# Self attention: the exponentials of four key blocks added on VectorE, one ones-matmul group for each sum

## The chip, the cores and the metric

The kernel runs on one core of one Trainium2 chip (trn2). The metric is device time in microseconds for one execution, the median of three runs; lower is better. Engines are named as in the profile: PE is TensorE's matmul, PEld its weight load, DVE VectorE, ACT ScalarE, POOL GpSimd, SP SyncE.

## What is computed

The reference is a decoder layer stack on x of shape (4, 512, 512): a self attention with rotary embedding, token-routed experts, a quantised MLP, a second self attention, a cross attention over a context and a last linear layer. Only the two self attentions matter here; each has 16 heads of 32 and runs for 4 batch elements of 512 tokens. Cut to that:

```python
q, k, v = (heads of a linear layer of layernorm(x))      # (4, 16, 512, 32) each
attn  = jnp.einsum('bhqd,bhkd->bhqk', q, k) * Dh ** -0.5 # the first one with rotary q and k
probs = jax.nn.softmax(attn, axis=-1)
out   = jnp.einsum('bhqk,bhkd->bhqd', probs, v)
x     = x + out.transpose(0, 2, 1, 3).reshape(B, S, D) @ out_w.T + out_b
```

The kernel computes exp(score - maximum), multiplies it by v without normalising, sums it over the keys, and multiplies the context by the reciprocal of the sum. The change is in how that sum over 512 keys is formed.

## The kernel before

Class `Attention` builds both self attentions (`rope` true for the first) and the cross attention (`cross`). All engines run their own instruction stream and meet at semaphores; the order on each engine is written out by hand. A batch element goes through projections (PE, with pieces of the maximum search planned between them), the output projection of the element before, the value projection, and then the stretch that this text calls the heads: `pe_heads` on PE, the loop over `u` in `act_batch` on ACT, `dve_self_heads` on DVE.

The heads are 16 units u, u = 4 g + kb: a group g of four heads (HG = 4) and one of T = 4 blocks of 128 keys. For a unit PE makes the scores of four heads (L1075, keys on the partitions), ACT takes their exponentials in two halves of 128x1024 fp32 (L1224, into one of three buffers `p(u)`), and PE multiplies them by the values (`pe_values`, L883), one unit behind. Keys lie on the partitions, so the sum over them takes a matmul with a matrix of ones (`pe_sum`, L897, four heads side by side into PSUM bank 7). Because that is fp32 work, DVE first adds the exponentials of two neighbouring units (`dve_add`, L1468, two halves) into one tile `pair_sum`, and `pe_pair_sum` takes the ones-matmul of the pair: two of them, accumulated, make a group's sum. A `pe_sum` is eight PE instructions in the trace.

Around a group's end the order is as follows. DVE adds at odd u. PE takes the first pair at kb = 3 and the second at kb = 1 of the next group, after the scores of that unit and the values of the one before; at the last group it comes after the next batch element's first projection, and in the last element right after the heads. Then DVE reads the sums by a transpose (`dve_read_sums`, L1319), before its add of the same unit; at kb = 2 it inverts and transposes them back (L1324, L1326) and multiplies the context (L1336); ACT and POOL split the result into a high and a low half (L1145, L1595). DVE also holds, at fixed units, the layer norm of the next element (L183, L194, L201), the low half of its transposed tiles (L1296, after units 8, 10, 12, 14), the transposed maxima (L1291) and, in the last element, weight splits (L456).

`pair_sum` is one buffer, so an add waits until the ones-matmul of the pair before has read it (`pair_read`); the exponential of u waits until the buffer of u - 3 has been added and multiplied by the values (`act_wait_block`).

Of the kernel before, what the change touches and what calls it, by code (L numbers as in the profile page):

```python
# [15 lines left out]
NB = 4  # L16
S = 512
D = 512
NH = 16
HD = D // NH  # L20
T = S // P
C = D // P
# [21 lines left out]
ALU = mybir.AluOpType  # L44
# [118 lines left out]
def slot(ap, i):  # L163

    return ap[:, bass.ds(i, 1), :].rearrange("p a n -> p (a n)")
# [72 lines left out]
class Phase:  # L238
# [22 lines left out]
    def pe(self, pe): pass  # L261
# [6 lines left out]
class Start(Phase):  # L268
# [56 lines left out]
    def pe(self, pe):  # L325
        m = self.m
        pe.wait_ge(*self.at(self.own_made, 1))
        pe.wait_ge(*self.at(self.memsets, 2))
        n = NE * NB * T
        pe.matmul(m.ps[:, 0, 0:n], self.tri, flat(self.own), start=True, stop=True)  # L330
        pe.matmul(m.ps[:, 1, 0:n], self.ones, flat(self.own), start=True, stop=True).then_inc(self.counted, 1)
        for i in range(T):
            pe.wait_ge(*self.at(self.norm.xn_ready, i + 1))
            self.following.pe_turn_x(pe, i, None)

        pe.wait_ge(*self.at(self.copied, 1))
        self.following.pe_first_chunk(pe)
# [143 lines left out]
class Attention(Phase):  # L481
# [15 lines left out]
    def __init__(self, m, name, mats, bufs, early, q_bias, k_bias, v_bias, out_bias, rope=False, cross=False):  # L497
# [24 lines left out]
        s = self.sem  # L522
# [66 lines left out]
        own = not cross  # L589
        self.out_full, self.out_free, self.out_added = s("out_full", own * NB * T), s("out_free", own * (NB - 1) * T), s("out_added", own * NB * T)  # L590
        self.values_done = s("values_done", own * NB * NH)
        self.paired, self.pair_read = s("pairs_added", own * NB * self.ADDS * 2), s("pair_sums_read", own * NB * self.ADDS)
        self.qs_ready = s("sin_part", rope * NB * self.NPROJ)
        self.sums_read, self.reciprocals, self.inverted = s("sums_read", NB * C), s("reciprocals", NB * C), s("sums_inverted", NB * C)
        self.normed, self.ch, self.cl = (s(n, NB * C) for n in ("ctx_normed", "ctx_high", "ctx_low"))
# [38 lines left out]


    PAIRS = HG * T // 2
    ADDS = NH // 2
    WITH_PROJ = ("", "", ",pp", ",pp", "p,pp", "p,pp", "m,pp", ",pp")
    WITH_OUT = (",pp", ",pp", "m,pp", "p,pp")
    WITH_V = ("p,pp", "m,pp", ",pp", ",pp")  # L640
# [260 lines left out]
    def pe_sums(self, pe, u, b):  # L901


        if self.cross:
            if u:
                self.pe_sum(pe, self.p(u - 1), u % T == 1, u % T == 0).then_inc(self.pv_done, 1)
        elif u < NH and u % T == T - 1:
            self.pe_pair_sum(pe, u // 2 - 1, b)
        elif T < u < NH and u % T == 1:
            self.pe_pair_sum(pe, (u - T) // 2 + 1, b)  # L910

    def pe_pair_sum(self, pe, n, b):
        if n % 2 == 0 and n:
            pe.wait_ge(*self.at(self.sums_read, b * C + n // 2))
        pe.wait_ge(*self.at(self.paired, 2 * (b * self.ADDS + n + 1)))
        self.pe_sum(pe, self.pair_sum, n % 2 == 0, n % 2 == 1).then_inc(self.pair_read, 1)

    def pe_proj(self, pe, n, b):
        m = self.m
# [15 lines left out]
    def pe(self, pe):  # L935
        if self.cross:
            self.pe_cross(pe)
            return
        if not self.rope:
            for i in range(T):  # L940
                self.pe_turn_x(pe, i, None)
            self.pe_first_chunk(pe)
        if self.rope:
            pe.wait_ge(*self.at(self.const, self.nconst))
        self.pe_batch(pe, 0)
        with pe.Fori(1, NB - self.rope) as b:
            self.pe_batch(pe, b)
        if self.rope:
            self.pe_batch(pe, NB - 1)
            self.pe_pair_sum(pe, self.ADDS - 1, NB - 1)  # L950
            self.pe_last_out(pe)
            return
        self.pe_pair_sum(pe, self.ADDS - 1, NB - 1)

        for c in range(C):
            if c == 0:
                pe.wait_ge(*self.at(self.cl, NB * C - 1))
            if c == C - 1:
                pe.wait_ge(*self.at(self.cl, NB * C))
            for i in range(T):  # L960
                last = self.pe_out(pe, i, [c])
                if c == C - 1:
                    last.then_inc(self.out_full, 1)
# [22 lines left out]
    def pe_batch(self, pe, b):  # L986
        first = first_of(b)
        self.of_batch(b)
        if not first:
            pe.wait_ge(*self.at(self.slot_free[0], self.slot_count(0, b)))  # L990
        for n in range(self.NPROJ):
            if n or not first:
                self.pe_proj(pe, n, b)
            if n == 0 and not first:
                self.pe_pair_sum(pe, self.ADDS - 1, b - 1)
            if self.rope and n:
                self.pe_rotate(pe, n - 1, b)
            self.pe_planned(pe, b, "proj", n, 1)
        if self.rope:
            self.pe_rotate(pe, self.NPROJ - 1, b)  # L1000
        if not first:
            self.weights.wait(pe, 3)
            pe.wait_ge(*self.at(self.cl, b * C))
            for i in range(T):
                self.wait_free(pe, ("v", i), b)
                self.pe_out(pe, i, [0, 1])
                self.pe_planned(pe, b, "out", i, 0)
                self.pe_out(pe, i, [2, 3]).then_inc(self.out_full, 1)
                self.pe_planned(pe, b, "out", i, 1)
        self.pe_project_values(pe, b)  # L1010
        self.pe_heads(pe, b)
# [89 lines left out]
    def act_wait_chunks(self, act, n, b):  # L1101

        if n < 2 and not self.cross and not first_of(b):
            if n == 0:
                act.wait_ge(*self.at(self.values_done, b * NH))
                act.wait_ge(*self.at(self.paired, 2 * b * self.ADDS))
            else:
                act.wait_ge(*self.at(self.pair_read, b * self.ADDS))

    def act_audio(self, act, n, c):  # L1110
        act.wait_ge(*self.at(self.audio_loaded, n * 16 + 16))
# [137 lines left out]
    def act_wait_block(self, act, u, h, b):  # L1249

        before = u - 3
        if u == 2:
            for half in range(2):
                act.wait_ge(*self.at(self.stacked[half], (b + 1) * 24 * 16))
        if before >= 0:
            act.wait_ge(*self.at(self.values_done, b * NH + before + 1))
            act.wait_ge(*self.at(self.paired, 2 * (b * self.ADDS + before // 2) + h + 1))

    def act_next(self, act, u):

# [50 lines left out]
    def dve_read_sums(self, v, g, b):  # L1311


        if self.cross:
            v.wait_ge(*self.at(self.pv_done, b * NH + T * (g + 1)))
        else:
            v.wait_ge(*self.at(self.pair_read, b * self.ADDS + 2 * g + 2))
        v.wait_ge(*self.at(self.normed, b * C + g))
        v.transpose(self.sums, self.m.ps[:, 7, :]).then_inc(self.sums_read, 1)  # L1319

# [135 lines left out]
                self.dve_planned(v, b, "v", i, step)  # L1456
        self.dve_self_heads(v, b)

    def dve_add(self, v, n, b):

        if n == 0:
            for half in range(2):
                v.wait_ge(*self.at(self.stacked[half], (b + 1) * 24 * 16))
        v.wait_ge(*self.at(self.pair_read, b * self.ADDS + n))
        for h in range(2):
            cols = slice(2 * h * S, (2 * h + 2) * S)
            v.wait_ge(*self.at(self.exp_done[h], b * NH + 2 * n + 2))
            v.tensor_tensor(self.pair_sum[:, cols], self.p(2 * n)[:, cols], self.p(2 * n + 1)[:, cols], ALU.add).then_inc(self.paired, 1)  # L1468

    def dve_self_heads(self, v, b):  # L1470
        m = self.m
        first = first_of(b)
        nb = (b + 1) % NB
        own = lambda i: slot(m.x, nb * T + i)
        for u in range(NH):
            g, kb = divmod(u, T)
            self.dve_planned(v, b, u - 1, 3)
            for step in range(3):
                self.dve_planned(v, b, u, step)
            if g and kb == 1:  # L1480
                self.dve_read_sums(v, g - 1, b)
            if u % 2:
                self.dve_add(v, u // 2, b)
            if g and kb == 2:
                self.dve_multiply(v, g - 1, b)
            if self.of_last(b):
                self.dve_next(v, u)
            if u == (3 if self.rope else 0) and not self.without_next(b):
                if self.rope:
                    v.wait_ge(*m.x_all)  # L1490
                self.norm.dve_stats(v, own, (0, 1))
            if u == (4 if self.rope else 0) and not self.without_next(b):
                self.norm.dve_stats(v, own, (2, 3))
                self.norm.dve_aggregate(v, b)
            if self.rope and not first:
                if u == 0:
                    self.dve_final_moments(v, b - 1)
                if u == 2:
                    self.dve_final_apply(v, b - 1)
            for i in range(T):  # L1500
                if not self.without_next(b) and u == ((6, 6, 8, 8) if self.rope else (4, 4, 6, 6))[i]:
                    self.norm.dve_apply(v, b, own, lambda i: m.xn[:, i, :], [i])
# [226 lines left out]
def first_of(b):  # L1729

    return isinstance(b, int) and b == 0
# [890 lines left out]
```

## Time and profile before

| | us |
|---|---|
| median of three runs | 1719.95 (1714.42 to 1724.76) |
| the profiled execution | 1716.46 |
| its span, first to last instruction | 1714.5 |
| busy in the span: PE / DVE / ACT / POOL | 1489.2 / 1261.1 / 871.7 / 530.4 |
| mean granted TensorE clock, share of full | 0.958 |

Busy time is the union of an engine's instructions; PE's matmuls are pipelined and their ends modelled. The idle time in a row is that of the engine just before the instruction, with what ended it behind the arrow. The profiled execution lies 3.5 us below the median of the runs.

### The profile page before, as it was taken

How to read it: one execution, taken by the hardware profiler on the slowest of the kernel's cores; microseconds unless marked ns; L12 is line 12 of the kernel's file. 1: busy time of each engine (PE TensorE's matmuls, PEld its weight loads, DVE VectorE, ACT ScalarE, POOL GpSimd, SP SyncE). 2: the span in 40 equal slices, each digit the busy share in tenths (PEclk: the TensorE clock that was granted, in tenths of full speed). 3: DMA queues.
4: the chain of work that ended last, by engine and by line, in shares of the span. 5: the costliest groups of instructions: out<-in, count | busy, mean ns of one | idle time of the engine just before them, and what ended most of it. 6: DMA issues, size and time to landing. Idle time of an engine off the chain costs nothing. (4 is left out here: it accounts for less than half of the span.)

```text
span 1714.5 us, 26624 instructions
## 1 busy us (share of the span) xinstructions
PE 1489.2 (87%) x8760; PEld 577.9 (34%) x8761; DVE 1261.1 (74%) x1783; ACT 871.7 (51%) x1071; POOL 530.4 (31%) x450
## 2 busy tenths in 40 slices
PE   3789999999959994688798999999999999999948
PEld 1223323233236661344332323333242323323213
DVE  4687897878855556888687788788945776768675
ACT  2245273452822333788737455463837454563735
POOL 1625447355420004422141322323131321414130
PEclk9889999999979997899998999999999999999979
DMA  5241202103313446300230201212031120303002
GB/s 196 74 122 32 68 25 52 47 0 75 119 54 111 147 135 137 54 1 0 62 74 1 54 22 31 84 65 65 25 91 33 45 53 24 73 0 92 12 0 99
DMA packets 82776, 105.40 MB, mean 61 GB/s; under 512 B 14096, under 2 KB 56208, under 8 KB 82576
## 3 DMA queue, kind: packets, MB, share of 16 engines
q1 hardware_dynamic: 79120, 96.10, 19.3%
q0 software_dynamic: 3584, 8.39, 2.3%
q8 instruction: 39, 0.64, 0.2%
q14 instruction: 33, 0.27, 0.1%
HBM read 48.21 MB, written 18.35 MB: 39 GB/s over the span
## 5 line engine op out<-in xcount | busy, mean ns | idle before, releaser
L1224 ACT ACTIVATE arena<-ps 128x1024 f32<-128x1024 f32 x384 | 373.4, 1026 | 108.4 <-PE ps L1075 98.0
L1284 DVE TENSOR_REDUCE arena<-ps 128x2 f32<-128x1024 f32 x256 | 299.7, 1220 | 56.2 <-PE ps L828 56.0
L468 PE MATMUL ps<-xt,w 128*128 128x512 f16 (+1 forms) x1872 | 295.3, 308 | 7.6 <-DVE w L456 3.8
L1075 PE MATMUL ps<-arena 97*128 97x512 f16 (+1 forms) x768 | 211.8, 389 | 14.8 <-ACT arena L1224 10.6
L883 PE MATMUL ps<-arena 128*32 128x512 f32 x1536 | 208.5, 615 | 15.3 <-DVE arena L1319 8.7
L468 PEld LDWEIGHTS ps<-xt,w 128*128 128x128 f16 (+1 forms) x1872 | 151.4, 99 | 141.7 <-issue 36.5
L468 PE MATMUL ps<-w,arena 128*128 128x512 f16 (+1 forms) x804 | 185.5, 381 | 12.7 <-issue 12.7
L1468 DVE TENSOR_TENSOR arena<-arena 128x1024 f32<-128x1024 f32 x128 | 175.2, 1408 | 11.8 <-PE ps L897 9.9
L1725 POOL TENSOR_TENSOR arena<-arena 128x512 f16<-128x512 f32 x96 | 116.6, 1216 | 158.3 <-ACT arena L1204 148.4
L1199 ACT ACTIVATE arena<-ps,arena 128x512 f32<-128x512 f32 x96 | 65.9, 687 | 182.2 <-PE ps L468 171.9
L1581 DVE TENSOR_SCALAR arena<-arena 128x1024 f32<-128x1024 f32 x128 | 106.7, 839 | 68.4 <-ACT arena L1224 67.9
L897 PE MATMUL ps<-arena 128*32 128x512 f32 x1024 | 138.0, 610 | 12.6 <-DVE arena L1468 11.8
L1595 POOL TENSOR_TENSOR arena<-arena 128x512 f16<-128x512 f32 x36 | 56.4, 1566 | 276.5 <-ACT arena L1145 276.5
L1075 PEld LDWEIGHTS ps<-arena 97*128 97x128 f16 (+1 forms) x768 | 59.2, 98 | 198.2 <-issue 100.9
L468 PEld LDWEIGHTS ps<-w,arena 128*128 128x128 f16 x804 | 75.7, 98 | 108.6 <-issue 30.5
L1135 ACT ACTIVATE arena<-ps 128x512 f32<-128x512 f32 x48 | 28.7, 597 | 136.7 <-PE ps L468 136.7
L468 PE MATMUL ps<-w,xt 128*128 128x512 f16 x384 | 92.0, 380 | 0.0
L828 PE MATMUL ps<-arena 32*128 32x512 f16 x512 | 70.0, 394 | 23.9 <-DVE arena L1284 21.7
L2071 PE MATMUL ps<-arena 128*128 128x512 f16 x256 | 63.3, 401 | 27.7 <-ACT arena L2089 27.7
L201 DVE TENSOR_SCALAR xn<-x,mv,rstd 128x512 f32 (+1 forms) x76 | 63.6, 890 | 24.4 <-POOL rstd L214 24.4
L2053 PE MATMUL ps<-arena,xt 128*128 128x512 f16 x256 | 61.9, 399 | 14.1 <-DVE arena L2212 9.4
L211 POOL TENSOR_TENSOR rstd<-mv,eps 128x4 f32<-128x4 f32 x27 | 9.8, 363 | 189.1 <-DVE mv L194 180.1
(217 smaller groups left out, 2001.5 us busy)
## 6 DMA issues: line engine op xcount, KB each, us to landing
arena<-arena SPq DMA_DIRECT2D x576, 64.0 KB, 2.0
raw<-in_ffn_parts SPq DMA_DIRECT2D x16, 512.0 KB, 3.8
raw<-in_ctxT SPq DMA_DIRECT2D x7, 1024.0 KB, 5.2
sorted_x<-arena SPq DMA_DIRECT2D x1, 4864.0 KB, 17.2
arena<-sorted_x SPq DMA_DIRECT2D x19, 256.0 KB, 3.7
sorted_y<-arena SPq DMA_DIRECT2D x19, 256.0 KB, 2.1
out<-x SPq DMA_DIRECT2D x16, 256.0 KB, 2.0
x<-in_x SPq DMA_DIRECT2D x1, 3072.0 KB, 12.0
```

Source lines behind the costliest of these rows:

```text
L201: v.tensor_scalar(dst(i), src(i), m.mv[:, i, 0:1], m.rstd[:, i:i + 1], ALU.subtract, ALU.mult).then_inc(self.xn_ready, 1)
L468: last = pe.matmul(out, left[l](cl[k]), right[r](cr[k]), start=start and k == 0 and a == 0, stop=stop and k == n - 1 and a == 2)
L828: last = pe.matmul(banks[:, k, :], self.qf[rows, 1, 0, g, t * P:(t + 1) * P], self.qf[rows, 0, 0, g, :], start=True, stop=True, tile_posit ...
L883: last = pe.matmul(self.context(g)[HD * j:HD * (j + 1)], self.v[:, kb, HD * (HG * g + j):HD * (HG * g + j + 1)], self.p(u)[:, j * S:(j + 1 ...
L897: last = pe.matmul(self.m.ps[HD * j:HD * (j + 1), 7, :], self.ones, p[:, j * S:(j + 1) * S], start=start, stop=stop, tile_position=(0, HD ...
L1075: last = pe.matmul(self.m.ps[:, j4, :], self.kst[0:R, HG * g + j4, kb * P:(kb + 1) * P], self.qst[0:R, HG * g + j4, :], start=True, stop=True)
L1199: act.activation(self.qb[:, n % 2, :], self.bank(item), ACT.Identity, scale=s, bias=self.pb[:, C * w + c:C * w + c + 1]).then_inc(self.ban ...
L1224: act.activation(self.p(u)[:, 2 * h * S:(2 * h + 2) * S], flat(self.m.ps[:, 2 * h:2 * h + 2, :]), ACT.Exp, scale=SOFTMAX_SCALE).then_inc(s ...
L1284: v.tensor_reduce(self.mx[:, g % 2, j:j + 2, t:t + 1].rearrange("p h t -> p (h t)"), self.slot_banks(item, b), AX.X, ALU.max).then_inc(sel ...
L1468: v.tensor_tensor(self.pair_sum[:, cols], self.p(2 * n)[:, cols], self.p(2 * n + 1)[:, cols], ALU.add).then_inc(self.paired, 1)
L1581: v.tensor_scalar(p, p, slot_col(self.hi, b * T + kb), CLIP_LOW, ALU.min, ALU.max).then_inc(self.clipped[h], 1)
L1725: g.tensor_tensor(self.qf[:, w, 1, c, :], src[:, n % 2, :], self.qf[:, w, 0, c, :], ALU.subtract).then_inc(self.fl, 1)
```

## The change

DVE adds all four units of a group: at kb = 1 the exponentials of units 4 g and 4 g + 1 go into `pair_sum`, at kb = 2 and kb = 3 those of the unit are added to `pair_sum` in place. PE takes one ones-matmul per group (start and stop both set), at the place where the second pair's stood. The new helper `added` counts the adds up to a unit; the waits of ACT and DVE follow it. The cross attention is left as it is.

```diff
     PAIRS = HG * T // 2
-    ADDS = NH // 2
+    ADDS = (T - 1) * C
...
-        elif u < NH and u % T == T - 1:
-            self.pe_pair_sum(pe, u // 2 - 1, b)
         elif T < u < NH and u % T == 1:
-            self.pe_pair_sum(pe, (u - T) // 2 + 1, b)
-
-    def pe_pair_sum(self, pe, n, b):
-        if n % 2 == 0 and n:
-            pe.wait_ge(*self.at(self.sums_read, b * C + n // 2))
-        pe.wait_ge(*self.at(self.paired, 2 * (b * self.ADDS + n + 1)))
-        self.pe_sum(pe, self.pair_sum, n % 2 == 0, n % 2 == 1).then_inc(self.pair_read, 1)
+            self.pe_group_sum(pe, u // T - 1, b)
+
+    def pe_group_sum(self, pe, g, b):
+        if g:
+            pe.wait_ge(*self.at(self.sums_read, b * C + g))
+        pe.wait_ge(*self.at(self.paired, 2 * (b * self.ADDS + (T - 1) * (g + 1))))
+        self.pe_sum(pe, self.pair_sum, True, True).then_inc(self.pair_read, 1)
...
-            act.wait_ge(*self.at(self.paired, 2 * (b * self.ADDS + before // 2) + h + 1))
+            act.wait_ge(*self.at(self.paired, 2 * self.added(before, b) + h + 1))
...
-    def dve_add(self, v, n, b):
-
-        if n == 0:
+    def added(self, u, b):
+
+        return b * self.ADDS + (T - 1) * (u // T) + max(u % T - 1, 0)
+
+    def dve_add(self, v, u, b):
+
+        if u == 1:
             for half in range(2):
                 v.wait_ge(*self.at(self.stacked[half], (b + 1) * 24 * 16))
-        v.wait_ge(*self.at(self.pair_read, b * self.ADDS + n))
+        if u % T == 1:
+            v.wait_ge(*self.at(self.pair_read, b * C + u // T))
         for h in range(2):
             cols = slice(2 * h * S, (2 * h + 2) * S)
-            v.wait_ge(*self.at(self.exp_done[h], b * NH + 2 * n + 2))
-            v.tensor_tensor(self.pair_sum[:, cols], self.p(2 * n)[:, cols], self.p(2 * n + 1)[:, cols], ALU.add).then_inc(self.paired, 1)
+            v.wait_ge(*self.at(self.exp_done[h], b * NH + u + 1))
+            if u % T > 1:
+                v.wait_ge(*self.at(self.paired, 2 * (self.added(u, b) - 1) + h + 1))
+            v.tensor_tensor(self.pair_sum[:, cols], self.p(u - 1)[:, cols] if u % T == 1 else self.pair_sum[:, cols],
+                            self.p(u)[:, cols], ALU.add).then_inc(self.paired, 1)
...
-            if u % 2:
-                self.dve_add(v, u // 2, b)
+            if kb:
+                self.dve_add(v, u, b)
```

The remaining edits rename the last sum of a batch element (`pe_pair_sum(ADDS - 1, b)` becomes `pe_group_sum(C - 1, b)`) and count `pair_read` by groups.

## Rows read from the trace of the kernel before

**Rows 1.** The page, part 1: busy us, share of the span, instructions of each engine.
```profile
PE 1489.2 (87%) x8760; PEld 577.9 (34%) x8761; DVE 1261.1 (74%) x1783; ACT 871.7 (51%) x1071; POOL 530.4 (31%) x450
```

**Rows 2.** Windows, DVE: stretch, its length, DVE busy (instructions), clock, DMA share, GB/s.
```profile
110.49:153.69 43.20, 35.29 (x47) 0.96 0.35 117
217.79:263.13 45.34, 40.52 (x52) 0.96 0.07 24
327.23:372.41 45.18, 40.52 (x52) 0.96 0.06 23
436.84:480.61 43.77, 37.17 (x41) 0.97 0.36 121
911.13:953.55 42.42, 32.69 (x37) 0.99 0.00 1
1009.84:1049.65 39.81, 32.61 (x37) 1.00 0.01 1
1104.82:1144.76 39.94, 32.62 (x37) 1.00 0.29 105
1200.07:1242.85 42.78, 40.64 (x45) 1.00 0.08 25
```

**Rows 3.** Groups by form: busy us, mean ns of one, idle before and its releasers.
```profile
L1468 DVE TENSOR_TENSOR arena<-arena 128x1024 f32<-128x1024 f32 x128 | 175.2, 1408 | 11.8 <-PE ps L897 9.9 <-ACT arena L1224 1.1 <-issue 0.5
L897 PE MATMUL ps<-arena 128*32 128x512 f32 x1024 | 138.0, 610 | 12.6 <-DVE arena L1468 11.8 <-issue 0.8
```

**Rows 4.** Timeline, DVE, one group (start us, us, instructions merged, idle before, releaser).
```profile
1124.26 0.72 DVE L1319 STREAM_TRANSPOSE arena<-ps 128x512 f32<-128x512 f32 x1 [0.80 <-PE ps L897]
1124.90 2.32 DVE L1468 TENSOR_TENSOR arena<-arena 128x1024 f32<-128x1024 f32 x2
1127.13 0.25 DVE L1324 RECIPROCAL arena<-arena 128x16 f32<-128x16 f32 x1
...
1129.53 3.34 DVE L1468 TENSOR_TENSOR arena<-arena 128x1024 f32<-128x1024 f32 x2
1132.79 0.68 DVE L1296 TENSOR_TENSOR xt<-ps,xt 128x512 f16<-128x512 f32 x1
1134.81 0.72 DVE L1319 STREAM_TRANSPOSE arena<-ps 128x512 f32<-128x512 f32 x1 [1.34 <-PE ps L897]
```

**Rows 5.** Timeline, POOL, in the same group.
```profile
1129.85 1.94 POOL L1595 TENSOR_TENSOR arena<-arena 128x512 f16<-128x512 f32 x1 [9.21 <-ACT arena L1145]
```

**Rows 6.** Timeline, PE: a ones-matmul and the scores behind it.
```profile
1117.88 1.04 PE L897 MATMUL ps<-arena 128*32 128x512 f32 x8
1118.85 1.04 PE L1075 MATMUL ps<-arena 97*128 97x512 f16 x4
```

**Rows 7.** Timeline, DVE, start of the heads of the second attention's third element.
```profile
1104.82 2.37 DVE L1468 TENSOR_TENSOR arena<-arena 128x1024 f32<-128x1024 f32 x2
...
1108.93 2.36 DVE L1468 TENSOR_TENSOR arena<-arena 128x1024 f32<-128x1024 f32 x2 [1.54 <-PE ps L897]
...
1114.05 0.72 DVE L1319 STREAM_TRANSPOSE arena<-ps 128x512 f32<-128x512 f32 x1 [1.84 <-PE ps L897]
```

**Rows 8.** Timeline, DVE, start of the heads of the second attention's first element.
```profile
914.77 0.28 DVE L1291 TENSOR_SCALAR arena<-ps 16x128 f16<-16x128 f32 x1 [1.29 <-PE ps L839]
917.66 2.36 DVE L1468 TENSOR_TENSOR arena<-arena 128x1024 f32<-128x1024 f32 x2 [2.61 <-PE ps L897]
...
922.69 0.72 DVE L1319 STREAM_TRANSPOSE arena<-ps 128x512 f32<-128x512 f32 x1 [1.75 <-PE ps L897]
```

**Rows 9.** Timeline, PE: two long waits of a ones-matmul for DVE.
```profile
239.77 1.85 PE L897 MATMUL ps<-arena 128*32 128x512 f32 x8 [2.77 <-DVE arena L1468]
...
1241.71 1.07 PE L897 MATMUL ps<-arena 128*32 128x512 f32 x8 [2.83 <-DVE arena L1468]
```

**Rows 10.** Windows, all engines (PE, PEld, DVE, ACT, POOL): what follows a stretch of heads.
```profile
1144.80:1195.00 50.20, 49.32 (x253) 18.57 (x251) 38.90 (x39) 14.77 (x24) 19.20 (x16) 1.00 0.26 63
```

More of the change, by code:

```diff
@@ L591, in __init__ @@
         self.values_done = s("values_done", own * NB * NH)
-        self.paired, self.pair_read = s("pairs_added", own * NB * self.ADDS * 2), s("pair_sums_read", own * NB * self.ADDS)
+        self.paired, self.pair_read = s("pairs_added", own * NB * self.ADDS * 2), s("pair_sums_read", own * NB * C)
         self.qs_ready = s("sin_part", rope * NB * self.NPROJ)
@@ L949, in pe @@
             self.pe_batch(pe, NB - 1)
-            self.pe_pair_sum(pe, self.ADDS - 1, NB - 1)
+            self.pe_group_sum(pe, C - 1, NB - 1)
             self.pe_last_out(pe)
             return
-        self.pe_pair_sum(pe, self.ADDS - 1, NB - 1)
+        self.pe_group_sum(pe, C - 1, NB - 1)
         for c in range(C):
@@ L994, in pe_batch @@
             if n == 0 and not first:
-                self.pe_pair_sum(pe, self.ADDS - 1, b - 1)
+                self.pe_group_sum(pe, C - 1, b - 1)
             if self.rope and n:
@@ L1107, in act_wait_chunks @@
             else:
-                act.wait_ge(*self.at(self.pair_read, b * self.ADDS))
+                act.wait_ge(*self.at(self.pair_read, b * C))
     def act_audio(self, act, n, c):
@@ L1316, in dve_read_sums @@
         else:
-            v.wait_ge(*self.at(self.pair_read, b * self.ADDS + 2 * g + 2))
+            v.wait_ge(*self.at(self.pair_read, b * C + g + 1))
         v.wait_ge(*self.at(self.normed, b * C + g))
```

## Prediction

> **What bounds the kernel now.** I read the page's busy table first: PE is busy for 87% of the span, DVE for 74% [rows 1]. Taken alone that says that work moved from PE to DVE is a gain. But the change touches only the eight stretches of heads, four in each self attention, so I cut these out: each window runs from DVE's first add of a batch element to its reading of the fourth group's sums [rows 2]. In this order of time they are the first attention's elements 0 to 3 and the second's 0 to 3. The reader is to compare length and DVE busy: 342.4 us in all, of which DVE works 292.0 (the sums of both columns). Its idle time is 7.9, 4.8, 4.7, 6.6, 9.7, 7.2, 7.3 and 2.1 us, 50.4 together. DVE stands at 85% here, not 74%.
>
> Next the groups by form: one half add means 1408 ns, 128 of them in all, and an add already ended 11.8 us of idle time of PE in front of ones-matmuls [rows 3]. So the coupling between the engines is DVE's add, PE's ones-matmul, DVE's read. Then the timeline of one group of four units [rows 4]: from one reading of the sums to the next 10.55 us (1124.26 to 1134.81), in which DVE waits only at the end, for PE's ones-matmul. PE is without a gap there and is what sets that period; DVE has 1.34 us left beside it.
>
> **What is removed.** Per batch element PE takes 4 ones-matmul calls in place of 8. Their price on PE is the distance from the call to the scores behind it, 1118.85 - 1117.88 = 0.97 us [rows 6]. It comes to 4 x 0.97 = 3.9 us per element, 8 x 3.9 = 31 us in all. This is a gain only where PE sets the period. The group above would go from 10.55 to 9.58 us on PE.
>
> **What is added.** DVE makes 12 adds of two halves per element in place of 8. Two halves cost 1127.13 - 1124.90 = 2.23 us from start to start when nothing is beside them [rows 4]; I take 2.24, so 4 x 2.24 = 8.96 us per element and 71.7 us in all. The other end is the mean with everything that happens beside it, 2 x 1.408 = 2.82 us [rows 3], which is 18.5 us more for 32 adds. I take the lower one because of what the difference consists of: the add at kb = 3 takes 3.34 us where a POOL instruction of 1.94 us runs beside it [rows 4, 5], and the change gives POOL no further instruction. The same ones will meet an add as now. The adds in place read the tile that they write; their new wait is for the same half of the unit before, with the other half's add between, so I cost it at nothing. Without that cover it would be one more of the small gaps below, which come to 0.44 us for a whole element.
>
> **What DVE's idle time can take up.** The added work fills idle time first. What can't be filled:
> - Behind the last add of a group DVE waits for PE to start the ones-matmul, run it and signal. The add of 1129.53 ended at 1132.87; in that group PE came late (the sums are read at 1134.81). Where PE stands ready, its call takes 1.04 to 1.07 us [rows 6, 9], and with the start and the signal I take 1.40 us. What DVE has to do in that time (0.6 us of a transposed tile's low half [rows 4], 0.9 us of the layer norm's, a weight split) counts as cover, so 0.8, 0.5 or 0 remains of it.
> - Short gaps between dependent DVE instructions, 0.44 us per element: what is left of 7.3 us once its waits are named.
> - At an element's start the exponentials are not there yet.
>
> Element by element, new length = DVE busy + 8.96 + idle time that stays:
> - Second attention, elements 1 and 2: the waits of 1.54 and most of 1.84 us [rows 7] are filled by the adds of units 2 and 6. What stays is 0.5 + 0.8 + 0.8 + 1.4 + 0.44 = 3.9. So 32.62 + 8.96 + 3.9 = 45.5 against 39.94, +5.6, and +5.7 for element 1.
> - Second attention, element 0: its first group is paced by exponentials, and DVE waits 1.29, 2.61 and 1.75 us [rows 8]. The group can end only 0.97 earlier, by the one ones-matmul that PE loses in it, so of 5.65 us 5.65 - 2.24 - 0.97 = 2.4 stay; with 0.8 + 0.8 + 1.4 + 0.44, 5.9. So 32.69 + 8.96 + 5.9 = 47.6 against 42.42, +5.1. First attention, element 0: alike, but the statistics of the layer norm cover the first wait and its application the second; 4.0 stay, +5.1.
> - First attention, elements 1 and 2: 0.8 + 1.4 + 0.44 = 2.6 stay. 40.52 + 8.96 + 2.6 = 52.1, +6.8 and +6.9.
> - First attention, element 3: no next layer norm, weight splits cover two groups' waits: 1.4 + 1.4 + 0.3 + 0.44 = 3.5 stay, 49.6 against 43.77, +5.9.
> - Second attention, element 3: DVE is busy 40.64 of 42.78 us, nearly nothing is left. 1.6 stay, 51.2, +8.4.
>
> The sum is 5.1 + 6.8 + 6.9 + 5.9 + 5.1 + 5.7 + 5.6 + 8.4 = 49.5 us. PE's 31 us are in it already: they turn into waiting, since its 9.58 us per group now stand beside some 12.2 of DVE (10.55 + 2.24 of a third add, less the 0.54 by which the wait at the group's end shrinks to 1.40).
>
> **Who waits for it.** Queued behind PE's wait for the last add are the scores of the unit after next, the values and, at an element's end, the whole next projection phase. That phase takes no delay back: PE is busy for 49.32 of its 50.20 us, and DVE for 38.90 [rows 10]. ACT isn't what ends late: an exponential waits for the adds of three units before, which the change doesn't put later in order, and for the second unit of a group it asks for the add of kb = 2 where it asked for the pair's. The sums' tile is read at the same place as now.
>
> **The clock.** PE will wait some 2.6 us once per group instead of working through. Today such a wait of 2.77 us is followed by a ones-matmul of 1.85 us, that is at the lower of its two levels (1.2 GHz), and one of 2.83 us by one of 1.07 us at 2.4 GHz [rows 9]. The windows show it as 0.97 against 1.00 [rows 2]. At the lower level each sum puts 1.85 - 1.04 = 0.8 us on DVE's path. There are 32 of them, of which the first group's eight hardly wait, so 24 x 0.8 = 19 us at most. And what PE does behind an element's last sum would be slower; if it lost at each of the eight ends as much as two such calls, 1.6 us, that is 13. Between 0 and 32 I take 6, nearer to the lower end, because one of the two waits shown was followed by the full clock, and because a call at half speed is late only where DVE stands waiting for it.
>
> **The rivals.**
> 1. PE bounds the heads, and DVE's added work disappears beside it: -31 us, 1685. For it speaks the busy table, and that the exponentials have three buffers, so that adds may lag behind. It decides as long as DVE's group with its three adds stays under PE's 9.6 us. Against it: DVE's 32.6 to 40.6 us of work plus 8.96 are longer than seven of the eight windows as they are now, before any wait is counted (the eighth, the second attention's element 0, has 41.7 against 42.4). Read plainly, the Trainium skill is on this rival's side: "Perfetto Trace Analysis", section "Identifying the Most-Contended Engine", says to improve the engine with the highest occupancy, which is PE here. The same section excepts TensorE, whose matmul busy share it calls no good measure of how near the engine is to its limit; the windows agree with the exception, since DVE's share is 85% where the change works.
> 2. The backlog is partly hidden: PE and ACT run ahead through the buffers inside an element, and only what is left at its end counts. Then the elements with 7 us of idle time lose about 2, those with less their full sum: roughly +25, 1741. Against it: each ones-matmul stands in PE's order in front of the next scores, so a group's delay is passed on.
> 3. The clock falls at almost every group: +49.5 + 32, 1798.
> 4. Adds meet POOL more often than now, at the mean price: +49.5 + 18.5 + 6, 1790.
> That the edit doesn't do what it says I leave aside: each add and wait is counted through one helper.
>
> **How the numbers follow.** 1716.5 of the profiled execution + 49.5 + 6 = 1772.0. That execution lies 3.5 below the median of the runs, so I put the new median a little above, at 1773. Chances: forecast (1758 to 1785) 0.70, rival 3 with rival 4 (over 1785) 0.13, rival 2 0.10, rival 1 0.04, no difference by some balance of both 0.03. The range 1752 to 1796 leaves out rivals 1 and most of 2, and the far end of 3. Slower by over 0.5%, about what a measurement of this kernel can tell from no change: 0.93; within it 0.03; faster 0.04.
>
> **What would show it.** Right: L1468 has 192 instructions at about 1.4 us, some 80 us more in all; L897 has 768; the eight windows last some 395 us together in place of 342; DVE is over 90% busy in them; PE waits for L1468 in front of L897 some 50 us or more, where it now waits 12; the projection phase keeps its 50.2 us. Wrong: if PE still has no gap in a group of the second attention, the forecast fails at its base. If the windows grow by 50 us and the total doesn't, a delay was taken back behind them. If half adds are shorter than 1.17 us or their pairs closer than 2.2, the price was too high; if L897 shows many calls at 1.85 us, the clock's term was too low.

## The result

The changed kernel takes 1776.74 us (median of four runs, 1774.22 to 1779.04) beside 1718.03 for the kernel before (four runs): ratio 1.035, 95% interval 1.033 to 1.037. The profiled execution took 1776.69 us, its span is 1774.9. The forecast was 1773, slower.

The page's first part and the groups of DVE's adds and PE's ones-matmuls answer to [rows 1, 3]:

```profile
span 1774.9 us, 26262 instructions
...
PE 1498.0 (84%) x8504; PEld 571.6 (32%) x8505; DVE 1330.0 (75%) x1847; ACT 870.3 (49%) x1071; POOL 533.5 (30%) x450
```
```profile
L1473 DVE TENSOR_TENSOR arena<-arena 128x1024 f32<-128x1024 f32 x192 | 247.9, 1342 | 3.4 <-ACT arena L1222 3.4
...
L897 PE MATMUL ps<-arena 128*32 128x512 f32 x768 | 107.8, 632 | 16.1 <-DVE arena L1473 16.0
```

DVE has 64 half adds more, at a lower mean (1342 ns) than before (1408). What they take above the shortest of them (1171 ns, before 1174) is 33 us together where it was 30, so an estimate from these means says that they lose to POOL about what they lost before, spread over more adds. PE has a quarter of its ones-matmuls less and yet is busy 8.8 us longer; its mean granted clock went from 0.958 to 0.939, and an instruction of its ones-matmuls takes up to 1.8 times as long as the shortest (1062 ns against 589).

The eight windows, cut as in [rows 2] from the first add of a batch element to the reading of the fourth group's sums (stretch, length, DVE busy, clock, DMA share, GB/s):

```profile
112.45:161.08 48.63, 44.21 (x54) 0.94 0.31 104
225.25:277.39 52.14, 48.26 (x60) 0.91 0.06 21
341.57:393.89 52.32, 48.28 (x60) 0.91 0.05 20
458.33:511.95 53.62, 46.56 (x49) 0.85 0.30 99
943.62:990.71 47.09, 41.47 (x45) 0.99 0.00 1
1046.19:1093.95 47.76, 41.37 (x47) 0.93 0.00 1
1148.99:1196.07 47.08, 41.38 (x47) 0.93 0.25 89
1251.13:1304.08 52.95, 49.59 (x55) 0.89 0.06 20
sum 401.59, DVE 361.12; mean DVE 45.14
```

The same windows over all engines, before and after (the sums alone):

```profile
sum 342.44, PE 324.74 PEld 85.82 DVE 292.04 ACT 260.62 POOL 100.58; mean PE 40.59 PEld 10.73 DVE 36.50 ACT 32.58 POOL 12.57
sum 401.59, PE 330.50 PEld 79.47 DVE 361.12 ACT 261.74 POOL 105.42; mean PE 41.31 PEld 9.93 DVE 45.14 ACT 32.72 POOL 13.18
```

PE was the fuller engine in them before, 95% against DVE's 85%, and its idle time there has gone from 17.7 to 71.1 us: what the change takes from PE has turned into waiting.

They last 401.6 us together where they lasted 342.4, so 59.2 of the 60.4 us by which the span grew lie in them. The other 1.2 us come from the start: the first add stands at 112.45 in place of 110.49, where neither kernel has done anything that differs, and behind the windows 0.7 us less pass than before. What follows a stretch takes hardly anything back: the window that answers to [rows 10], again 50.20 us long, has PE busy for 49.33.

```profile
1196.10:1246.30 50.20, 49.33 (x253) 18.56 (x251) 38.89 (x39) 14.76 (x24) 19.20 (x16) 1.00 0.26 63
```

Window by window the growth was 5.4, 6.8, 7.1, 9.9, 4.7, 8.0, 7.1 and 10.2 us against 5.1, 6.8, 6.9, 5.9, 5.1, 5.7, 5.6 and 8.4 in the prediction. Four fit within 0.45 us, and four are larger, by 9.5 us together.

One group in which DVE hardly stands still, on DVE (timeline; it answers to [rows 4]): from reading to reading 12.01 us where it was 10.55.

```profile
1170.92 0.72 DVE L1317 STREAM_TRANSPOSE arena<-ps 128x512 f32<-128x512 f32 x1 [1.84 <-PE ps L897]
1171.56 4.59 DVE L1473 TENSOR_TENSOR arena<-arena 128x1024 f32<-128x1024 f32 x4
...
1178.37 3.31 DVE L1473 TENSOR_TENSOR arena<-arena 128x1024 f32<-128x1024 f32 x2
1181.60 0.68 DVE L1294 TENSOR_TENSOR xt<-ps,xt 128x512 f16<-128x512 f32 x1
1182.93 0.72 DVE L1317 STREAM_TRANSPOSE arena<-ps 128x512 f32<-128x512 f32 x1 [0.65 <-PE ps L897]
```

The reader is to see that the third add stands next to the second with no gap, and that the last add ends at 1178.37 + 3.31 = 1181.68 and the sums are read 1.25 us later, where 1.40 was put down. The period is that of the forecast (some 12.2). PE's waiting is not where the forecast had it: its ones-matmul starts at 1181.82 without a wait, because PE had waited earlier in the group, 1.03 us of it for the low half (L1294):

```profile
1178.58 0.65 PE L854 MATMUL ps<-ident,xn 128*128 128x128 f32 x4 [1.03 <-DVE xt L1294]
...
1181.82 1.04 PE L897 MATMUL ps<-arena 128*32 128x512 f32 x8
```

And the first of the DVE rows shows a wait of 1.84 us in the group before, where 0.8 was expected. Where that came from took the experiments.

### The profile page after: what moved, and what is told of

The parts are those of the page before. It is cut to its first block and busy times, and to the rows that moved or that the text cites. A ratio compares the mean times of both kernels' runs of the same rounds, so it can differ in the third digit from the quotient of the medians.

```text
span 1774.9 us, 26262 instructions
## 1 busy us (share of the span) xinstructions
PE 1498.0 (84%) x8504; PEld 571.6 (32%) x8505; DVE 1330.0 (75%) x1847; ACT 870.3 (49%) x1071; POOL 533.5 (30%) x450
## 5 line engine op out<-in xcount | busy, mean ns | idle before, releaser
L468 PE MATMUL ps<-xt,w 128*128 128x512 f16 (+1 forms) x1872 | 298.4, 310 | 16.4 <-DVE xt L1294 10.1
L1073 PE MATMUL ps<-arena 97*128 97x512 f16 (+1 forms) x768 | 224.5, 404 | 34.8 <-ACT arena L1222 31.5
L1473 DVE TENSOR_TENSOR arena<-arena 128x1024 f32<-128x1024 f32 x192 | 247.9, 1342 | 3.4 <-ACT arena L1222 3.4
L883 PE MATMUL ps<-arena 128*32 128x512 f32 x1536 | 218.7, 643 | 21.5 <-DVE arena L1317 8.7
L1073 PEld LDWEIGHTS ps<-arena 97*128 97x128 f16 (+1 forms) x768 | 56.9, 100 | 234.0 <-issue 110.3
L897 PE MATMUL ps<-arena 128*32 128x512 f32 x768 | 107.8, 632 | 16.1 <-DVE arena L1473 16.0
L468 PEld LDWEIGHTS ps<-w,arena 128*128 128x128 f16 x804 | 76.3, 99 | 110.7 <-issue 33.8
L1143 ACT ACTIVATE arena<-arena 128x512 f16<-128x512 f32 x48 | 30.2, 629 | 87.2 <-DVE arena L1334 87.2
```

Of the source, the lines that this page charges most:

```text
L468: last = pe.matmul(out, left[l](cl[k]), right[r](cr[k]), start=start and k == 0 and a == 0, stop=stop and k == n - 1 and a == 2)
L883: last = pe.matmul(self.context(g)[HD * j:HD * (j + 1)], self.v[:, kb, HD * (HG * g + j):HD * (HG * g + j + 1)], self.p(u)[:, j * S:(j + 1 ...
L897: last = pe.matmul(self.m.ps[HD * j:HD * (j + 1), 7, :], self.ones, p[:, j * S:(j + 1) * S], start=start, stop=stop, tile_position=(0, HD ...
L1073: last = pe.matmul(self.m.ps[:, j4, :], self.kst[0:R, HG * g + j4, kb * P:(kb + 1) * P], self.qst[0:R, HG * g + j4, :], start=True, stop=True)
L1473: v.tensor_tensor(self.pair_sum[:, cols], self.p(u - 1)[:, cols] if u % T == 1 else self.pair_sum[:, cols], self.p(u)[:, cols], ALU.add).t ...
```

## The experiments

The theory: DVE's added work is the loss, and PE's saving turns into waiting. Its rivals: the new form itself (one sum per group, adding in place) costs; PE's saving is real and hides larger costs; the clock does it. What the windows grew beyond the sum was a question of its own.

### Without the third add

```diff
-    ADDS = (T - 1) * C
+    ADDS = (T - 2) * C
...
-            if kb:
+            if kb % 2:
                 self.dve_add(v, u, b)
```

> The changed kernel without the add at kb = 2: the third key block's exponentials are left out of the sums (and the self attentions' exponentials take a quarter of their scale, so that no sum is zero). DVE then has as many adds as the kernel before, PE one ones-matmul per group as the changed one. Theory (the added 2.24 us of DVE per group are the whole loss): the loss goes and a part of PE's saving shows, 1718 - 15, so 1697 to 1711. Rival (PE's saving is worth its full 31 us once the adds are gone): 1687. Rival (the loss comes from the new form, one sum per group and its waits): above 1745.

It took 1714.14 us, ratio 0.998 (0.997 to 0.999). The 59 us go with the add, so neither the form nor the single sum costs anything. The other finding was outside the theory's range of 1697 to 1711: PE's saving of 31 us, alone on top of DVE's old work, is worth some 2.5 us (1 to 5 by the interval). Its windows, in the same columns, last 340.0 us together, 2.4 less than before, and one of them has grown by 4.7 us, the first attention's element 3:

```profile
437.64:486.08 48.44, 41.11 (x42) 0.89 0.32 109
...
sum 340.03, DVE 293.89; mean DVE 36.74
```

DVE's timeline in it and POOL's:

```profile
451.62 7.66 DVE L1473 TENSOR_TENSOR arena<-arena 128x1024 f32<-128x1024 f32 x2
461.42 0.72 DVE L1317 STREAM_TRANSPOSE arena<-ps 128x512 f32<-128x512 f32 x1 [2.14 <-PE ps L897]
```
```profile
450.97 4.98 POOL L1698 TENSOR_TENSOR x<-x,arena 128x512 f32<-128x512 f32 x4
455.92 1.14 POOL L1601 TENSOR_TENSOR arena<-arena 128x512 f16<-128x512 f32 x1
```

Two half adds took 7.66 us in place of 2.3. They lie beside five POOL instructions, which took 1.1 to 1.25 us each, and the first of the two ended only at 458.1, 1 us behind POOL's last (457.06). Without this meeting I estimate the saving at some 7 us (2.5 + 4.7). The other seven windows together are 7.1 us shorter, still far from 31. A group of the second attention takes 10.0 us, where PE alone would need 9.6, and in its fourth group, as long as before (10.0 us), the last values now wait 0.78 us for ACT's exponentials. I read this as DVE's old work and ACT following PE closely; no run separates the two.

### Half of the third add

```diff
-            cols = slice(2 * h * S, (2 * h + 2) * S)
+            cols = slice(2 * h * S, (2 * h + 1 + (u % T != 2)) * S)
```

> The changed kernel with the add at kb = 2 cut to half its columns (512 in place of 1024 in each of its two instructions; half of the third block's exponentials are left out of the sums). Theory (time follows DVE's work): 2 x 512 columns at about 1.04 ns less per group, 32 groups, -34 us, so 1738 to 1748. Rival (a fixed cost of one more step with its waits): 1770 or more. Rival (another engine takes over soon): the time of the first experiment already, 1700 to 1710.

1737.85 us, ratio 1.012 (1.010 to 1.014). From no third add to half of it the time rises by 23.7 us, from half to all of it by 38.9. Both steps add 32 x 2 x 512 columns, 34 us by the rule that DVE's work is the time. In the windows of the three profiles DVE's busy time goes from 293.9 to 331.1 and 361.1, so by 37.2 and 30.0, since the half-width adds are instructions more in the first step and only wider in the second. Its idle time goes from 46.1 to 33.9 and back to 40.5. So the first step is smaller than its work, since part of it fills idle time, and the second is larger than its work. That is the same surplus as in the windows, and ACT's wait for the multiplication grows along with it, from 35.8 to 60.6 and 87.2 us.

### PE's work as before, DVE's as after

```diff
     def pe_group_sum(self, pe, g, b):
         if g:
             pe.wait_ge(*self.at(self.sums_read, b * C + g))
+        self.pe_sum(pe, self.p(T * g + T - 1), True, True)
         pe.wait_ge(*self.at(self.paired, 2 * (b * self.ADDS + (T - 1) * (g + 1))))
```

> The changed kernel with one more ones-matmul call per group on PE, ahead of its wait for the adds and overwritten by the real one: the adds of the changed kernel with PE's work of the kernel before. Theory (PE's saving was spent on waiting): the call fits into the wait, 1775 to 1784. Rival (PE's 31 us were saved and the adds cost 90): 1808. Rival (the TensorE clock's lower level in PE's waits costs the time): the call shortens the waits, the granted clock rises from 0.94 and the time falls by 5 to 10 us, to 1767 to 1772.

1781.14 us, ratio 1.037 (1.035 to 1.038), so 4.4 us above the changed kernel, or 3 by the two ratios, whose intervals overlap. Beside three adds the 31 us of ones-matmuls are worth 3 to 4, which rules out the rival of 1808. The granted clock rose from 0.939 to 0.949 and the time didn't fall. That speaks against the clock as a main cause, though not cleanly, because the call also takes PE's time.

### Adds not in place

```diff
-            v.tensor_tensor(self.pair_sum[:, cols], self.p(u - 1)[:, cols] if u % T == 1 else self.pair_sum[:, cols],
+            v.tensor_tensor(self.pair_sum[:, cols], self.p(u - 1)[:, cols] if u % T == 1 else self.p(u)[:, cols],
                             self.p(u)[:, cols], ALU.add).then_inc(self.paired, 1)
```

> The changed kernel with the adds at kb = 2 and kb = 3 reading the unit's exponentials twice and not the tile that they write; their waits stay (the sums are then those of the last block alone, twice; the self attentions' exponentials take a quarter of their scale). Theory (adding in place costs nothing): 1774 to 1780. Rival (reading what was just written costs 0.1 us or more per half add): 64 adds of two halves less 0.1 each, 1764 or less.

1779.84 us, ratio 1.036 (1.034 to 1.038), 3 above the changed kernel and not below it. The eight windows last 401.4 us together, as in the changed kernel (401.6); the rest of the span is 3.6 us longer, although nothing in it differs. Reading the tile that was just written costs nothing that shows.

### Two orders meant to take the surplus back

Where does the surplus of 9.5 us come from? In the changed kernel the row of 1.84 us above stands behind this on ACT, PE and DVE (timelines):

```profile
1160.89 1.02 ACT L1222 ACTIVATE arena<-ps 128x1024 f32<-128x1024 f32 x1
1164.37 0.63 ACT L1143 ACTIVATE arena<-arena 128x512 f16<-128x512 f32 x1 [2.46 <-DVE arena L1334]
1164.90 1.92 ACT L1222 ACTIVATE arena<-ps 128x1024 f32<-128x1024 f32 x2
```
```profile
1165.96 0.60 PE L1073 MATMUL ps<-arena 97*128 97x512 f16 x2 [1.82 <-ACT arena L1222]
1166.88 1.03 PE L1073 MATMUL ps<-arena 97*128 97x512 f16 x2 [0.31 <-ACT arena L1222]
1167.84 1.94 PE L883 MATMUL ps<-arena 128*32 128x512 f32 x8
1169.55 1.29 PE L897 MATMUL ps<-arena 128*32 128x512 f32 x8
```

ACT's high half of the context (L1143) waits 2.46 us for DVE's multiplication (L1334), which now stands behind the third add. The exponentials of the next unit are queued behind it on ACT, the following scores behind those on PE, and the clock falls in PE's wait: values that take 1.06 us take 1.94. So the ones-matmul starts at 1169.55, 1.1 us after the last add has ended (1165.16 + 3.31 = 1168.47). Two moves follow from this reading and from a wait of PE's next projection for DVE's low half (L1294):

```diff
+            if g and kb == 2:
+                self.dve_multiply(v, g - 1, b)
             if kb:
                 self.dve_add(v, u, b)
-            if g and kb == 2:
-                self.dve_multiply(v, g - 1, b)
```
```diff
+        if not self.cross:
+            units = {{8: 7, 10: 9, 12: 11, 14: 13}.get(u, u): k for u, k in units.items()}
```

> The changed kernel with one order exchanged on DVE: at kb = 2 the multiplication of the last group's context stands before the add, not behind it. Nothing is added or left out. Theory (what the windows grew beyond the 49.5 us of the sum is ACT's wait for that multiplication, with the next exponentials and PE's scores queued behind it): 1 us back in two or three groups of most elements, 1766 to 1773. Rival (DVE's own work is the only bound): 1775 to 1779.

> The changed kernel with the four transposes of the next element's tiles planned one unit earlier (behind units 7, 9, 11, 13 in place of 8, 10, 12, 14), so that PE's next projection doesn't wait for DVE's low half of the last one. Theory (that wait, 1.5 us with a projection at the lower clock behind it, makes the element's last sum late): about 1 us back in each of six elements, 1769 to 1774. Rival (the wait is only moved, PE would wait for the last add anyway): 1775 to 1779.

> The changed kernel with both moves: multiplication before the third add, transposes one unit earlier. Theory (DVE's work is then all that is left, as the sum of the prediction has it): 1718 + 49.5, so 1763 to 1770, and a granted clock above 0.94. Rival (the order was not the matter): 1775 or more. Either way it stays above the kernel before by over 40 us, since no order takes an add away.

All three went the other way: 1788.48 us (ratio 1.041, 1.039 to 1.043), 1811.69 (1.054, 1.052 to 1.056) and 1800.90 (1.049, 1.046 to 1.051). With the multiplication first, the second attention's elements 1 and 2 did what was expected (their second groups fell from 13.65 and 13.52 to 12.27 us), but their last ones rose from 12.04 and 13.14 to 14.23 and 14.14, and the first attention's windows grew by 4.2, 3.6, 2.9 and 1.1 us more. The wait that was aimed at did shrink (ACT's for the multiplication from 87.2 to 43.3 us, PE's in front of the scores from 31.2 to 16.4). Others took its place: DVE is busy 5.9 us longer in the windows (367.0 us), and in the second attention PE waits 15.3 us for low halves where it waited 9.0. One reason is seen in the last element, DVE and PE:

```profile
1291.74 3.31 DVE L1473 TENSOR_TENSOR arena<-arena 128x1024 f32<-128x1024 f32 x2
1294.98 1.21 DVE L456 SCALAR_TENSOR_TENSOR w<-arena,w 128x1024 f16<-128x1024 f32 x1
1296.11 0.68 DVE L1294 TENSOR_TENSOR xt<-ps,xt 128x512 f16<-128x512 f32 x1
1296.71 2.34 DVE L1473 TENSOR_TENSOR arena<-arena 128x1024 f32<-128x1024 f32 x2
```
```profile
1296.92 1.11 PE L854 MATMUL ps<-ident,xn 128*128 128x128 f32 x4 [3.73 <-DVE xt L1294]
```

The meeting with POOL (3.31 us) moved from the last add to the third, and so in front of the low half that frees PE's slot. PE waits 3.73 us for it, with scores, values and the sum behind. With the transposes earlier (e6) it is the low half that stands in front of the multiplication. ACT and then PE wait longer for that, and DVE in the end for PE:

```profile
1210.39 0.60 PE L1075 MATMUL ps<-arena 97*128 97x512 f16 x2 [3.00 <-ACT arena L1224]
```
```profile
1216.13 0.72 DVE L1319 STREAM_TRANSPOSE arena<-ps 128x512 f32<-128x512 f32 x1 [4.03 <-PE ps L899]
```

So on DVE three instructions are waited for by others, the multiplication, the low half and the last add, and in none of the three orders was one of them early without another being late. So I turned to the engine that waits and has work queued behind its wait.

### ACT's wait moved behind an exponential

```diff
-            if kb == T - 1 and g:
+            if self.cross and kb == T - 1 and g:
                 self.act_context_high(act, g - 1, b)
+            if not self.cross and (kb == 0 and g > 1 or u == NH - 1):
+                self.act_context_high(act, g - 2 if kb == 0 else g - 1, b)
```

> The changed kernel with ACT's high half of a group's context (which waits for DVE's multiplication) behind the first unit's exponentials of the group after next in place of the last unit's of the next; DVE's order is as in the changed kernel. Theory (the second groups of 13.5 to 14.2 us are the loop multiplication, ACT's high half, the next exponentials, scores, sum): they come down to DVE's own 12.0 to 12.4 in the first attention's element 3 and the second's 1 and 2, 4 to 8 us in all, 1768 to 1773. Rival (another wait is equally late, or GpSimd's low half then meets another add): 1775 or more.

1764.43 us, ratio 1.029 (1.026 to 1.031): 12.3 us less than the changed kernel (10.5 by the two ratios), more than was expected. Of the 12.4 us by which the profiled span is shorter, 8.6 lie in the windows. Of the rest 1.8 lie ahead of the first add, where the two kernels do the same, so not all of the gain is the move's. ACT's wait for the multiplication, in the group of the high half (busy, mean ns, idle before it), in the changed kernel and in this one (before: 36.4 us):

```profile
L1143 ACT ACTIVATE arena<-arena 128x512 f16<-128x512 f32 x48 | 30.2, 629 | 87.2 <-DVE arena L1334 87.2
```
```profile
L1143 ACT ACTIVATE arena<-arena 128x512 f16<-128x512 f32 x48 | 30.2, 630 | 57.3 <-DVE arena L1336 57.3
```

PE's waits in front of the scores went from 11.2 us in the kernel before to 31.2 in the changed one and 14.6 here, and those in front of the ones-matmuls from 12.6 to 16.1 and 37.9:

```profile
L1073 PE MATMUL ps<-arena 97*128 97x512 f16 x512 | 156.8, 415 | 31.2 <-ACT arena L1222 29.0 <-DMA arena<-arena 1.2
```
```profile
L1073 PE MATMUL ps<-arena 97*128 97x512 f16 x512 | 152.9, 410 | 14.6 <-ACT arena L1222 11.8 <-DMA arena<-arena 1.4 <-issue 0.3
L897 PE MATMUL ps<-arena 128*32 128x512 f32 x768 | 106.8, 627 | 37.9 <-DVE arena L1475 37.8
```

PE now waits more where the forecast had it wait, if not for the 50 us that were named. In the group that ended with the 1.84 us above, its ones-matmul is behind 2.53 us (some 2.6 were forecast), and the adds, not ACT, are what it waits for:

```profile
1161.06 1.39 PE L897 MATMUL ps<-arena 128*32 128x512 f32 x8 [2.53 <-DVE arena L1475]
```

The eight windows here:

```profile
457.00:507.52 50.52, 46.61 (x49) 0.89 0.30 105
...
1042.08:1086.46 44.38, 40.42 (x46) 0.96 0.00 1
1141.50:1185.74 44.24, 40.43 (x46) 0.96 0.26 95
...
sum 392.99, DVE 359.83; mean DVE 44.98
```

393.0 us are 50.6 more than before; the sum of the prediction said 49.5. That they meet so closely is in part luck: DVE's idle time in them is 33.2 us, 7.3 less than in the changed kernel and still 5 above the 28 of the sum, and its busy time grew by 67.8 in place of 71.7. The second groups named in the expectation are at 12.22, 12.27 and 12.57 us, from 14.15, 13.65 and 13.52. The three elements that they belong to give 9.3 us, the other five together lose 0.7. DVE's busy time in the windows is 1.3 us less than in the changed kernel, so other meetings with POOL explain at most that much.

> The same move in the kernel before. Theory (there PE sets the period of a group and ACT's wait is not in its way): within 3 us of the kernel before. Rival (the move is worth what it is worth in the changed kernel, whatever the adds): 4 us or more less.

In the kernel before the same move is worth nothing: 1715.73 us, ratio 1.000 (0.999 to 1.001). The wait is there, but no one is late for it. The profile shows one thing more. The half adds became shorter (mean 1315 ns, from 1408), DVE's busy time in the windows fell from 292.0 to 283.7 us, and yet the windows last 342.1 us, as before (342.4). Before the change DVE's work was not what set the time.

### The change where DVE was idle

```diff
-            if u % 2:
+            if 1 < u < T and self.whole(b):
+                self.dve_add_on(v, u, b)
+            elif u % 2:
                 self.dve_add(v, u // 2, b)
```

Here `whole(b)` is true for the four elements, `dve_add_on` is the add in place, and PE leaves out the first group's first ones-matmul in them.

> The kernel before, with the change in the first group alone of the first attention's element 0 and of the second's elements 0, 1 and 2, where DVE waited in the trace of before and the changed kernel's first group was shorter (by 1.03, 0.88, 0.58 and 0.80 us). PE's loop over the second attention's elements ends one earlier and the last is written out. Theory (the change gains where DVE is idle and only there): 3 us less than before, 1713 to 1716 beside 1717, ratio 0.997 to 0.999. Rival (what the first group gains is given back in the next one): ratio 1.000.

1717.02 us, ratio 0.9995 (0.998 to 1.001). A gain of 3 us, 0.2%, can't be told from none here. Between the two profiled executions the first groups of the four elements were 0.8, 0.5 and 0.7 us shorter and once 0.3 longer, and the eight windows together were the same, 342.4 us. No version that computes everything beats the kernel before by more than this.

## Why the prediction was right

**The bound in the heads: right in its sum, not in its shares.** What told the outcome is that DVE's work and the added 8.96 us are longer than seven of the eight windows. Taking the third add away took the loss away, halving it gave 1737.85, just below its range of 1738 to 1748, and putting PE's work back cost 4 us of 31. DVE's 85% against the 87% of PE in the whole span did not tell it. The prediction never read PE's share in the same windows, and that is 95%: there too PE was the fuller engine, it set the period before the change (8.4 us less of DVE's work gained nothing in the kernel before with ACT's wait moved), and still taking work from it for DVE lost. So the windows do not bear out, as the prediction had it, the exception for TensorE in the Trainium skill ("Perfetto Trace Analysis", section "Identifying the Most-Contended Engine"). What fits the exception is another number: PE's matmul busy time rose by 8.8 us while its work fell.

**The add's price: right, a little high.** 8.96 us per element, 71.7 in all, were put down. DVE's busy time in the windows rose from 292.0 to 361.1, by 69.1. That POOL's collisions would stay as many held in the changed kernel (mean 1342 ns). It does not hold in general, as the 7.66 us in the kernel without the third add show and, the other way, the mean of 1315 ns in the kernel before with ACT's wait moved.

**DVE's idle time that stays: too small.** 28 us were to stay of 50.4 (342.4 + 49.5 - 292.0 - 71.7); 40.5 stayed (401.6 - 361.1). This is the term that was mis-sized.

**The step behind it that failed** is the sentence that ACT isn't what ends late. It looked at the waits that the change rewrites (those of the exponentials for the adds) and not at what stands on DVE behind the new instruction. The multiplication was moved 2.24 us back by the add at kb = 2, ACT waits for it in order, and the exponentials are queued behind that. Moving ACT's wait took 7.3 of the 12.3 us too much of idle time back and brought the windows within 1.1 us of the sum. Where the other 5 us stay was not found.

**The clock: the term is not confirmed as it was written.** 6 us were taken for late sums at the lower level. The windows' clock did fall (to 0.85 in one), and values and sums of 1.9 us stand in the rows above, but they followed PE's waits for ACT as much as those for DVE's last add. The kernel with ACT's wait moved has the windows' growth of the sum without the 6. A lower mean clock did not by itself make a window longer: the first attention's element 1 lasted 52.45 us at 0.85 there and 52.14 at 0.91 in the changed kernel. PE's scores (L1073, 97 rows) and values were busy 23 us longer over the whole changed kernel than before (156.8 + 218.7 against 143.9 + 208.5). How much of that is on the path, and so what the clock alone costs, was not separated.

**Nothing is taken back behind the windows: right**, but for 0.7 us. The 1.2 us outside of the windows come from the 2.0 by which the first add starts later, which the change does not explain: over the ten other profiles that start lies between 110.7 and 114.4.

**Signs named in advance.** The counts 192 and 768 and the projection phase came as written. The adds took 72.7 us more (some 80 were said), and DVE is busy for 89.9% of the windows (over 90). PE was to wait over 50 us for the adds in front of its ones-matmuls; it waited 16.1 on PE's rows, because it waited more in front of the scores (31.2). The windows were to last some 395 us and lasted 401.6.

**The total.** 1716.5 + 49.5 + 6 = 1772.0 against 1776.7 of the profiled execution: 4.7 us too low, made up of 9.7 more in the windows, 1.2 outside of them, 6 less for the clock's term and 0.2 of rounding. That it came so near is in part luck. The idle time was taken 12.3 us too low, and two terms stood against it: the adds, put 2.6 too high, and the 6 for the clock, which no run shows as a cost of its own.

## What to carry to other kernels

Before work is moved from the busiest engine to another, compare busy time plus added work with the length of the stretches in which it is moved; here that gave the sign. Comparing the two engines' busy shares gave the wrong one, over the whole span (87% against 74%) and in the stretches themselves (95% against 85%). Then go down the receiving engine's queue behind each new instruction and ask who waits for what comes later, and what is queued behind that waiter: a wait that cost nothing before (ACT's for the multiplication) closed a loop through DVE, ACT and PE. Where the receiving engine is full, exchanging its order made other results late here, and moving the wait on the engine that waits gave some 10 us back.

## What the runs showed of the hardware

Two half adds on DVE with two operands in SBUF took 7.66 us in place of 2.3 beside five POOL instructions of 6.1 us together, and the first of them ended 1 us behind the last of the five. In the changed kernel the same four POOL additions (L1698) took 7.09 us in place of 4.98, and DVE's add beside them 4.04. So such a meeting can fall on either engine, and it changed one window by 4.7 us between kernels whose instructions there are nearly the same; what decides it was not tested.
